# Loading an adjacency matrix transposed and checking it tile by tile in a four-layer graph kernel

## The chip, the core and the metric

The kernel runs on one core of a Trainium2 chip. The metric is the device time of one execution in microseconds (us), lower is better. The core has five engines, each with its own instruction stream: TensorE (PE; its weight loads are listed as PEld), VectorE (DVE), ScalarE (ACT), GpSimd (POOL) and SyncE (SP), which here issues all the DMAs. They meet only through semaphores. SBUF is the memory on the chip, with 128 partitions; PSUM is the memory that PE writes its products into, eight banks of 128x512 float32.

## What is computed

Four graph layers over `x` (8 graphs, 2048 nodes, 64 features) and one adjacency matrix `adj` (2048x2048), each with a residual and a layernorm. Cut to what matters:

```
# adj: 0/1 pattern with ones on the diagonal, each row divided by its sum
x = layernorm(x + L0(x, adj))   # x, A x and 2 A(A x) - x, mixed by weights made per node
x = layernorm(x + L1(x, adj))   # relu((A z) W), twice
x = layernorm(x + L2(x, adj))   # x Ws + (A x) Wn + bias
x = layernorm(x + L3(x, adj))   # [x, A x, 2A(Ax)-x, A x, 2A(Ax)-x] W + bias
```

All nonzero entries of row n are the same number r[n], the diagonal entry. So A is diag(r) times a 0/1 matrix, and the 0/1 matrix is exact in any format. Since this holds for the given matrix only, the kernel counts on the chip whether it does, and has a second, general body for any other matrix.

## The kernel before, in words

The eight graphs are four pairs j = 0..3 of 128 feature columns. A product of a pair with A is a pass p = 0..6 (0 and 1 for layer 0, 2 and 3 for layer 1, 4 for layer 2, 5 and 6 for layer 3). A pass has four chunks c of 512 nodes, a chunk is one PSUM bank: 16 blocks m of 128 nodes, for each a matmul of the high part and one of the low part of x (`xs`, split so that two fast fp32r matmuls give float32 accuracy) with the 0/1 matrix `B` (16 tiles of 128x2048). `mm` steps are quarters of a chunk, 8 matmuls. After a chunk DVE multiplies by `rrep`, which is r repeated over the partitions (step `scale`, L864); for p = 0 the result goes to memory (`y1d`) and, turned by four PE transposes (L571, step `after`) and copied by ACT (L727), back to the node-major form.

The **head** (L512 to L555 for PE and its counterparts `act_head`, `dve_head`, `pool_head`, `sp_head`) makes `B`. It loads `a` in 16 row tiles into four buffers, makes a 0/1 tile of each (`mb`: 768 columns on POOL, L983; 1280 on ACT, L674), turns it by 16 PE transposes (L530) and copies it from PSUM to `B` (ACT L693, DVE L813). DVE takes the diagonal (L798) and counts entries that differ from it (L803). `rrep` is made by matmuls with a matrix of ones (L545). Between the transposes PE makes pass 0 of pair 0 (128 matmuls, L559 and L560). At the end the counts are summed over the partitions by a matmul (L553), DVE writes `flag`, and every engine loads it and branches into `pe_main` and its counterparts.

Behind the branch every engine walks one list, `STEPS`, made by `order()` (L33) and written out by hand. It begins with the four `scale` and `after` steps of pass 0 of pair 0, which share one slot of `ring`, then `weights0` (the weights of layer 0, `Tw`), pass 1 of pair 0, and four quarters of pass 0 of pair 1. Then `opening(0)` prepares the operands of the per-node mixing of pair 0, and `weave` lays its 32 `T` steps (10 matmuls each, L653, and 8 DVE accumulations each, L965) among the quarters that pair 1 still has for layer 0: 28 of them, one between two `T` steps nearly everywhere. A `T` step takes one of two pairs of banks, so PE waits at a `T` until DVE has done the `T` before the last. Pairs 1, 2 and 3 follow in the same way, with the passes of the next pair among them, then the rest of the layers in two lanes.

Of the kernel before, what the change touches and what calls it, by code (L numbers as in the profile page):

```python
# [8 lines left out]
I32 = mybir.dt.int32  # L9
ALU = mybir.AluOpType  # L10
# [3 lines left out]
P = 128  # L14
# [7 lines left out]
NS = 768  # L22
# [10 lines left out]
def order():  # L33
# [5 lines left out]
    def one_pass(j, p):  # L39
# [12 lines left out]
        for c in range(NC):  # L52
            head = j == 0 and p == 0
            if not head:
                for m in range(4):
                    put("mm", j, p, c, m)
                    if c > 0 and p >= 2 and m == 0:
                        finish(c - 1)
                    if m < 3:
                        yield False  # L60
# [8 lines left out]
            if not head:  # L69
                yield True  # L70
# [72 lines left out]
    def layer0(j):  # L143
        yield from one_pass(j, 0)
        if j == 0:
            splits(j, 1)
            put("weights0")
        else:
            yield from split_ahead(j, 1)
        yield from one_pass(j, 1)  # L150

# [62 lines left out]
    for _ in layer0(0):  # L214
        pass
# [25 lines left out]


# [6 lines left out]
def gnn_stack(nc, xn, xt, a, at, emb, embt, b0, w01, w2, wbd, bias, eye, eps, out, zd, y1d, bd):  # L249
# [3 lines left out]
    with ctx:  # L253
# [5 lines left out]

        B = sb("B", [P, NT, N], F32R)  # L260
        with ExitStack() as scope:
            room = sb("room", [P, 2, N], F32, scope)
# [8 lines left out]
        r = sb("r", [P, NT], F32)  # L271
        cnt = sb("cnt", [P, NT], F32)
        neg = sb("neg", [P, NT], F32)
        sml = sb("sml", [P, 2, NC, 4, 8], F32)
        epst = sb("epst", [P, 1], F32)
        bad = sb("bad", [P, 1], F32)
        flag = sb("flag", [1, 1], I32)
        bias_t = sb("bias", [P, 2, C], F32)
        W1 = sb("W1", [P, 2, P], F32)
        with ExitStack() as scope:  # L280
            identb = sb("identb", [P, P], BF16, scope)
            onesf = sb("onesf", [P, P], F32, scope)
            mb0 = sb("mb0", [P, N], BF16, scope)
            astg = sb("astg", [P, N], F32, scope)
# [3 lines left out]
        with ExitStack() as scope:  # L288
            embn = sb("embn", [P, NT, DE], F32, scope)
            b0t = sb("b0t", [DE, C], F32, scope)  # L290
            with ExitStack() as inner:
                mb = [mb0, sb("mb1", [P, N], BF16, inner)]
            ring_x = sb("ring_x", [P, 2, 512], F32, scope)
# [4 lines left out]
        s_const, s_c2, s_w, s_x0, s_x1 = (sem(x) for x in ("const", "c2", "w", "x0", "x1"))  # L298
        s_a = [sem(f"a{i}") for i in range(4)]
        s_f = [sem(f"fetch{i}") for i in range(2)]  # L300
        s_p = sem("part")
        s_lx = [sem(f"loadx{i}") for i in range(2)]
        s_y1o = [sem(f"y1out{n}") for n in range(2)]
        s_z = [[sem(f"z{n}{c}") for c in range(NC)] for n in range(2)]
        s_re = [sem(f"reload{n}") for n in range(2)]
        s_out = [sem(f"out{n}") for n in range(2)]
        s_wl = sem("wload")
        s_e, s_bd = sem("embt"), sem("bd")
        s_g = [sem(f"g{i}") for i in range(2)]

        s_tr, s_rsum, s_sum, s_prod = sem("tr"), sem("rsum"), sem("sum"), sem("prod")
        s_turn, s_turny, s_four, s_b0, s_T = sem("turn"), sem("turny"), sem("four"), sem("b0"), sem("T")
        s_b0c = sem("b0copy")
        s_gmm = sem("gmm")

        s_signa, s_Ba, s_rrep, s_hi = sem("signa"), sem("Ba"), sem("rrep"), sem("hi")
        s_evict, s_sq, s_std, s_H, s_S, s_twh = (
            sem("evict"), sem("sq"), sem("std"), sem("H"), sem("S"), sem("twh"))
        s_gB = sem("gB")

        s_diag, s_cnt, s_Bd, s_lo, s_y, s_v = (
            sem("diag"), sem("cnt"), sem("Bd"), sem("lo"), sem("y"), sem("v"))
        s_flag, s_bad, s_chk = sem("flag"), sem("bad"), sem("chk")
        s_mean, s_var, s_norm, s_Lo, s_Sl = sem("mean"), sem("var"), sem("norm"), sem("Lo"), sem("Sl")
        s_acc, s_w0, s_twl, s_W = sem("acc"), sem("w0"), sem("twl"), sem("W")
        s_sum1, s_sum2, s_rec, s_Wc = sem("sum1"), sem("sum2"), sem("rec"), sem("Wc")
        s_ones_r, s_glo = sem("onesr"), sem("glo")

        s_ones, s_signp, s_join, s_pb = sem("ones"), sem("signp"), sem("join"), sem("pb")
# [3 lines left out]
        prod_at = {("prod", 0, 0, c): c + 1 for c in range(NC)}  # L333
        for s, v in numbered("mm", last=True).items():
            prod_at["prod", s.j, s.p, s.c] = v + 4
        split_at = {Step("split", j, 0, c): 4 * j + c + 1 for j in range(2) for c in range(NC)}
        split_at |= {s: v + 8 for s, v in numbered("split").items()}
        scale_at = numbered("scale")
        turn_at = numbered("ahead")
        turny_at = {s: i + 1 for i, s in enumerate(s for s in STEPS if s.kind == "after" and s.p in (0, 5))}  # L340
        four_at = {s: i + 1 for i, s in enumerate(s for s in STEPS if s.kind == "after" and s.p > 1)}
        evict_at = {s: i + 1 for i, s in enumerate(
            s for s in STEPS if s.kind == "ahead" or s.kind == "after" and s.p in (0, 2, 5))}
        v_at = {s: i + 1 for i, s in enumerate(s for s in STEPS if s.kind == "after" and s.p > 2)}
        pb_at = {s: i + 1 for i, s in enumerate(s for s in STEPS if s.kind == "after" and s.p in (4, 5))}
        T_at = numbered("T")
        join_at = numbered("join")
        prep_at = numbered("prep")
        prep2_at = {s: 2 * v for s, v in numbered("prep2").items()}
        mean_at, var_at, norm_at = numbered("centre"), numbered("deviate"), numbered("normed")  # L350
        n_T = len(T_at)

        def ahead(j, p, c):
            return Step("ahead", j, p, c)

        def after(j, p, c):
            return Step("after", j, p, c)


        load_at, load_after, slot_of = {}, {}, {}  # L360
        held, n_load = [None, None], [0, 0]
        for s in STEPS:
            if s.kind == "fetch" or s.kind == "part" and s.c % 2:
                i = s.p if s.kind == "fetch" else 1
                n_load[i] += 32 if s.kind == "fetch" else 16
                load_at[s], load_after[s], slot_of[s] = n_load[i], held[i], i
                held[i] = s


        bank_of, bank_after = {("prod", 0, 0, c): 4 + c for c in range(NC)}, {}  # L370
        turn, held = [0, 1], {}
        for i, s in enumerate(STEPS):
            if i == SECOND:
                turn = turn + [4, 5]
            if s.kind == "mm" and s.k == 0:
                b = turn.pop(0)
                turn.append(b)
                bank_of["prod", s.j, s.p, s.c], bank_after[s] = b, held.get(b)
                held[b] = Step("scale", s.j, s.p, s.c)
# [3 lines left out]
        nbank_of, nbank_after = {}, {}  # L383
        turn, held = [2, 3], {}

        def take(use, frees):
            b = turn.pop(0)
            turn.append(b)
            nbank_of[use], nbank_after[use] = b, held.get(b, (s_acc, 8 * n_T) if b > 3 else None)
            held[b] = frees  # L390

        for i, s in enumerate(STEPS):
            if i == SECOND:
                turn = turn + [6, 7]
            if s.kind == "ahead" or s.kind == "after" and s.p in (0, 5):
                take((s, "turn"), (s_evict, evict_at[s]))
            if s.kind == "after" and s.p == 2:
                take((s, "four"), (s_evict, evict_at[s]))
            if s.kind == "after" and s.p > 2:
                take((s, "four"), (s_v, v_at[s]))  # L400
# [3 lines left out]
        y_after, lx_at, lx_after, n_lx, n_y1o = {}, {}, {}, [0, 0], [0, 0]  # L404
        y1o_at = {}
        held = [[(s_rsum, 4)], [(s_rsum, 4)]]
        for s in STEPS:
# [9 lines left out]
            if s.kind == "loadx":  # L417
# [5 lines left out]
                elif s.j > 0:  # L423
                    lx_after[s] = (s_acc, 8 * T_at[Step("T", s.j - 1, 0, s.c + 2, 3)])
# [788 lines left out]
```

## Time and profile before

| | us |
|---|---|
| median of three runs | 1355.95 (1354.9 to 1357.07) |
| the profiled execution | 1359.67 |
| its span, first to last instruction | 1357.9 |
| PE busy | 1296.7 (95%) |
| DVE busy | 753.3 (55%) |
| ACT busy | 250.8 (18%) |
| POOL busy | 111.8 (8%) |

PE is busy 95% of the span, and 88% of the chain of work that ended last is PE's. The places where it isn't busy are read from stretches: a row of the table by stretches gives, for each engine, how long it was busy and with how many instructions, then the clock that TensorE was granted as a mean (1.00 is 2.4 GHz, 0.50 is 1.2 GHz), the share of the DMA engines and what they moved in GB/s. In the list in order of time a row is start, duration, engine, line, operation, output from inputs, shape, count, and in square brackets the idle time before it with what ended it.

### The profile page before, as it was taken

How to read it: one execution, taken by the hardware profiler on the slowest of the kernel's cores; microseconds unless marked ns; L12 is line 12 of the kernel's file. 1: busy time of each engine (PE TensorE's matmuls, PEld its weight loads, DVE VectorE, ACT ScalarE, POOL GpSimd, SP SyncE). 2: the span in 40 equal slices, each digit the busy share in tenths (PEclk: the TensorE clock that was granted, in tenths of full speed). 3: DMA queues.
4: the chain of work that ended last, by engine and by line, in shares of the span. 5: the costliest groups of instructions: out<-in, count | busy, mean ns of one | idle time of the engine just before them, and what ended most of it. 6: DMA issues, size and time to landing. Idle time of an engine off the chain costs nothing.

```text
span 1357.9 us, 16974 instructions
## 1 busy us (share of the span) xinstructions
PE 1296.7 (95%) x6314; PEld 1071.9 (79%) x6314; DVE 753.3 (55%) x1845; ACT 250.8 (18%) x433; POOL 111.8 (8%) x70
## 2 busy tenths in 40 slices
PE   6969999999999999799999999999999999999996
PEld 5758787778777888588888888888888888888885
DVE  6941677776777676866862453363135435334524
ACT  6730020111111120101111211121111211121211
POOL 5700000000000000000000101101000010010000
PEclk9979999999999999899999999999999999999998
DMA  8711111121112110100100000001001000000000
GB/s 303 290 58 39 27 56 36 47 73 36 47 35 74 36 59 24 47 28 20 39 14 1 1 1 0 1 8 55 1 9 55 0 1 1 1 1 0 32 1 34
DMA packets 25783, 54.06 MB, mean 40 GB/s; under 512 B 3024, under 2 KB 13776, under 8 KB 22992
## 3 DMA queue, kind: packets, MB, share of 16 engines
q1 hardware_dynamic: 25696, 52.90, 11.8%
q8 instruction: 54, 0.88, 0.3%
q14 instruction: 33, 0.27, 0.1%
HBM read 40.83 MB, written 12.06 MB: 39 GB/s over the span
## 4 chain that ended last, share of the span: by engine, by line
PE 88%; DVE 7%; DMA 2%; issue 1%; ACT 1%; POOL 1%; DVEq 0%; SPq 0%; ACTq 0%; POOLq 0%
PE ps L559 29%; PE ps L560 29%; PE ps L653 19%; PE ps L577 7%; PE ps L571 2%; DVE nat L965 1%; DVE ring L965 1%; DMA nat<-in_a 1%; DVE xs L875 1%; DVE xs L933 1%; DMA y1d<-ring 1%; PE ps L515 1%; POOL mb L983 1%; PE ps L530 0%; DVE nat L803 0%
## 5 line engine op out<-in xcount | busy, mean ns | idle before, releaser
L559 PE MATMUL ps<-B,xs 128*128 128x512 f32 x1792 | 712.3, 398 | 8.1 <-DVE xs L875 8.1
L560 PE MATMUL ps<-B,xs 128*128 128x512 f32 x1792 | 702.9, 392 | 0.0
L559 PEld LDWEIGHTS ps<-B,xs 128*128 128x128 f32 x1792 | 338.6, 189 | 78.4 <-issue 6.9
L560 PEld LDWEIGHTS ps<-B,xs 128*128 128x128 f32 x1792 | 338.7, 189 | 69.7
L653 PE MATMUL ps<-Tw,xs 128*128 128x512 f32 x1280 | 324.9, 402 | 15.3 <-DVE ring L965 7.8
L653 PEld LDWEIGHTS ps<-Tw,xs 128*128 128x128 f32 x1280 | 241.2, 191 | 77.7 <-DVE ring L965 9.7
L864 DVE TENSOR_TENSOR ring<-ps,rrep 128x512 f32<-128x512 f32 x96 | 66.3, 691 | 287.8 <-PE ps L560 275.6
L965 DVE SCALAR_TENSOR_TENSOR nat<-ps,embn,nat 128x128 f32<-128x128 f32 x448 | 154.1, 344 | 65.7 <-PE ps L653 65.7
L965 DVE SCALAR_TENSOR_TENSOR ring<-ps,embn,ring 128x128 f32<-128x128 f32 x512 | 175.5, 343 | 0.0
L577 PEld LDWEIGHTS ps<-W,ring 128*128 128x128 f32 x896 | 110.5, 191 | 7.0 <-DVE ring L864 2.6
L577 PE MATMUL ps<-W,ring 128*128 128x128 f32 x896 | 113.1, 275 | 1.7 <-DVE ring L864 1.7
L757 ACT ACTIVATE ring<-nat 128x512 f32<-128x512 f32 x60 | 37.9, 632 | 387.9 <-DVE nat L902 387.9
L1007 POOL TENSOR_TENSOR nat<-nat,bias 128x512 f32<-128x512 f32 x32 | 41.2, 1287 | 579.1 <-PE ps L571 579.1
L1000 POOL TENSOR_TENSOR nat<-nat,ring 128x512 f32<-128x512 f32 x16 | 23.6, 1476 | 596.9 <-DVE ring L965 596.9
L892 DVE TENSOR_TENSOR nat<-ps,nat 128x512 f32<-128x512 f32 x48 | 33.1, 690 | 66.6 <-PE ps L577 66.6
L965 DVE SCALAR_TENSOR_TENSOR nat<-ps,embn,ring 128x128 f32<-128x128 f32 x64 | 22.4, 350 | 79.5 <-PE ps L653 79.5
L762 ACT ACTIVATE sml<-sml,epst 128x8 f32<-128x8 f32 x64 | 19.3, 301 | 236.0 <-DVE sml L907 236.0
L752 ACT COPY ring<-ps 128x512 f32<-128x512 f32 x32 | 18.8, 587 | 177.4 <-PE ps L571 177.4
L875 DVE TENSOR_TENSOR xs<-nat,xs 128x512 fp32r<-128x512 f32 x64 | 40.2, 686 | 11.2 <-ACT xs L719 11.1
L902 DVE TENSOR_TENSOR nat<-nat,sml 128x512 f32<-128x512 f32 x64 | 44.4, 693 | 2.2
L912 DVE TENSOR_TENSOR nat<-nat,sml 128x512 f32<-128x512 f32 x64 | 44.3, 692 | 2.2
L907 DVE TENSOR_REDUCE sml<-ring 128x8 f32<-128x512 f32 x60 | 40.7, 678 | 8.4 <-ACT ring L757 8.4
(87 smaller groups left out, 601.3 us busy)
## 6 DMA issues: line engine op xcount, KB each, us to landing
room<-in_a SPq DMA_DIRECT2D x8, 1024.0 KB, 6.7
astg<-in_a SPq DMA_DIRECT2D x4, 1024.0 KB, 5.7
nat<-in_a SPq DMA_DIRECT2D x4, 1024.0 KB, 7.2
y1d<-ring SPq DMA_DIRECT2D x16, 256.0 KB, 2.4
ring<-in_xn SPq DMA_DIRECT2D x16, 256.0 KB, 2.9
ring_x<-in_xt SPq DMA_DIRECT2D x32, 128.0 KB, 3.2
ring_x<-y1d SPq DMA_DIRECT2D x32, 128.0 KB, 3.3
out<-nat SPq DMA_DIRECT2D x16, 256.0 KB, 2.4
```

The costliest lines, as they stand in the source:

```text
L559: pe.matmul(bank, x[:, 0, m, :], of, start=m == 0, stop=False)
L560: mm = pe.matmul(bank, x[:, 1, m, :], of, start=False, stop=ends and m == NT - 1)
L577: mm = pe.matmul(ps[:, bank, k * P:(k + 1) * P], src[:, k * P:(k + 1) * P], w, start=i == 0, stop=i == len(pairs) - 1)
L653: mm = pe.matmul(ps[:, 4 + 2 * p + q, :], src, Tw[:, wi, 512 * p:512 * p + 512], start=i == 0, stop=i == 4)
L757: ac.activation(square_slot(general, j, p, c), ch(nat[n], c), ACT.Square).then_inc(s_sq, 1)
L864: dv.tensor_tensor(to, ps[:, bank_of["prod", j, p, c], :], ch(rrep, 0 if general else c), ALU.mult).then_inc(s_y, 1)
L875: dv.tensor_tensor(lo, src, hi.bitcast(F32), ALU.subtract).then_inc(s_lo, 1)
L902: dv.tensor_tensor(g, g, sm[:, 1, :].unsqueeze(2).to_broadcast([P, 8, C]), ALU.subtract).then_inc(s_mean, 1)
L907: dv.tensor_reduce(sm[:, 2, :], q, axis=AX.X, op=ALU.add).then_inc(s_var, 1)
L912: dv.tensor_tensor(g, g, sm[:, 0, :].unsqueeze(2).to_broadcast([P, 8, C]), ALU.mult).then_inc(s_norm, 1)
L965: dv.scalar_tensor_tensor(sums[d % 2], ps[:, 4 + 2 * p:6 + 2 * p, i * C:(i + 1) * C], embn[:, t, d:d + 1], first[d] if d < 2 else sums[d % 2],
L1007: po.tensor_tensor(g, g, bias_t[:, p - 4, :].unsqueeze(1).to_broadcast([P, 8, C]), ALU.add).then_inc(s_pb, 1)
```

## The change

- **Loads.** The row tiles `a` are no longer an input. `adj.T` is loaded in 16 tiles `raw` into the place where `B` lies, without a wait between them. `rrep` and the diagonal come from the host as inputs of their own (`rb`, 1 MB, and `r16`). The pieces of x of pairs 0 and 1 are loaded ahead of every fourth tile.
- **Tile.** ACT counts the nonzero entries of a tile (Sign of its bits with `accum_out`); DVE compares the tile with `rrep`, writes the 0/1 result over it as `B` and counts the equal ones (`accum_out`). The transposes, the copies to `B`, POOL's part and the matmuls with ones are gone. The last tile is done in four pieces.
- **First products.** PE makes pass 0 of both pairs tile by tile in all eight banks: 16 matmuls for each tile. Chunks 2 and 3 of pair 1 are finished after tile 15, between the four `after` steps of pair 0. Each of the eight results has a slot of its own.
- **Outcome.** The difference of the two counts goes by DMA from a column to a row (`row<-bad`) while pass 1 of pair 0 runs; DVE writes `flag` after its eighth quarter, and all engines branch there.
- **Order.** `scale` and `after` of pair 1's pass 0 lie in pass 1 of pair 0, `weights0` behind the branch. Three quarters of pass 1 of pair 1 run ahead of the first `T`, and 13 are left to weave among the 32 `T` steps of pair 0.
- The general body starts from scratch and has semaphores of its own.

```diff
+    def head():
+        put("bias")
+        for m in range(NT):
+            if m % 4 == 0:
+                put("split", 0, 0, m // 4)
+                put("split", 1, 0, m // 4)
+            for c in range(NC if m == LAST else 1):
+                put("tile", 0, 0, c, m)
+            for j in range(2):
+                for c in range(NC if j == 0 else 2 if m >= 12 else NC):
+                    put("first", j, 0, c, m)
+            if m == LAST:
+                for c in range(NC):
+                    put("scale", 0, 0, c)
+        put("after", 0, 0, 0)
+        for m in range(12, NT):
+            put("first", 1, 0, 2, m)
...
+    def second_pass0():
+        products = one_pass(0, 1)
+        for i, _ in enumerate(products):
+            if i < 4:
+                put("scale", 1, 0, i)
+            if 2 <= i < 6:
+                put("after", 1, 0, i - 2)
+            if i == 7:
+                put("branch")
+                put("weights0")
+            if 8 <= i < 12:
+                put("split", 1, 1, i - 8)
...
-    products = layer0(1)
-    for _ in range(4):
-        next(products)
     put("loadx", 0, 0, 0)
     put("fetch", 0, 0, 0)
+    products = one_pass(1, 1)
+    for _ in range(3):
+        next(products)
     opening(0)
-    weave(0, products, 30, 2, 3)
+    weave(0, products, 13, 2, 3)
...
+                    if s.kind == "first" and not general:
+                        bank, of = ps[:, bank_of["prod", j, 0, c], :], B[:, k, c * 512:(c + 1) * 512]
+                        pe.wait_ge(s_B, tile_at[Step("tile", 0, 0, c if k == LAST else 0, k)])
...
+                        pe.matmul(bank, xs[n][:, 0, k, :], of, start=k == 0, stop=False)
+                        mm = pe.matmul(bank, xs[n][:, 1, k, :], of, start=False, stop=k == LAST)
...
+                        ac.activation(junk[:, tile_at[s] % 2, cols], raw[:, k, cols].bitcast(U32), ACT.Sign,
+                                      accum_out=cnt[:, 1, k + c:k + c + 1]).then_inc(s_nz, 1)
...
+                        dv.wait_ge(s_nz, tile_at[s])
+                        dv.scalar_tensor_tensor(B[:, k, cols], raw[:, k, cols], 1.0, rrep[:, cols], ALU.mult, ALU.is_equal,
+                                                accum_out=cnt[:, 0, k + c:k + c + 1]).then_inc(s_B, 1)
...
+                    if s.kind == "branch" and not general:
+                        dv.wait_ge(s_row, 16)
+                        dv.tensor_reduce(worst[:], row[:], axis=AX.X, op=ALU.max).then_inc(s_chk, 1)
+                        dv.wait_ge(s_chk, 3)
+                        dv.tensor_copy(flag[:], worst[:]).then_inc(s_flag, 1)
...
+                    if s.kind == "weights0":
+                        sp.wait_ge(s_y1o[0], 64)
+                        sp.wait_ge(s_turny, turny_at[after(0, 0, 3)])
+                        sp.dma_start(w01s, w01).then_inc(s_w, 16)
+                        sp.dma_start(w2s, w2).then_inc(s_w, 16)
```

What stands in a row at three places, first before and then with the change. **DVE at the end of the head**; `astg`, `nat` and `room` hold row tiles before, `raw` is a transposed tile, L803 and L816 are the counts:

```order
L798 SCALAR_TENSOR_TENSOR ring,r<-room,identf 128x128
L803 SCALAR_TENSOR_TENSOR room,cnt<-room,r,mb 128x2048
L813 CAST B<-ps 128x8x128
L818 TENSOR_TENSOR xs<-nat,xs 128x512 x4
L820 TENSOR_SCALAR neg<-r 128x16
L822 TENSOR_TENSOR cnt<-cnt,neg 128x16
L824 TENSOR_REDUCE bad<-cnt 128x1
```

```order
L854 TENSOR_TENSOR xs<-nat,xs 128x512 x2
L816 SCALAR_TENSOR_TENSOR B,cnt<-raw,rrep 128x2048 x3
L816 SCALAR_TENSOR_TENSOR B,cnt<-raw,rrep 128x512 x4
L842 TENSOR_TENSOR ring<-ps,rrep 128x512 x4
L854 TENSOR_TENSOR xs<-nat,xs 128x512 x4
L821 TENSOR_TENSOR odd<-cnt 128x19
```

Each tile now has one DVE instruction where it had two and, for every second tile, a copy (L813). The last tile has four short ones, and the scalings of pair 0 (L842) follow on them ahead of the sums for `flag`.

**DVE around the branch**, from the end of the head to the weights of layer 0 (`Tw`):

```order
L826 TENSOR_SCALAR bad<-ps 1x1
L828 CAST flag<-bad 1x1
L1145 TENSOR_LOAD flag
L1145 ISA x2
L1146 COMPARE_AND_BRANCH
L864 TENSOR_TENSOR ring<-ps,rrep 128x512 x4
L875 TENSOR_TENSOR xs<-nat,xs 128x512 x4
L916 TENSOR_TENSOR ring<-ring 64x1024
```

```order
L842 TENSOR_TENSOR ring_x<-ps,rrep 128x512
L842 TENSOR_TENSOR nat<-ps,rrep 128x512
L827 TENSOR_REDUCE worst<-row 1x1
L829 CAST flag<-worst 1x1
L1139 TENSOR_LOAD flag
L1139 ISA x2
L1140 COMPARE_AND_BRANCH
L895 TENSOR_TENSOR ring<-ring 64x1024
L897 TENSOR_SCALAR ring<-ring 128x1024
```

The scaling and splitting that stood behind the branch stand ahead of it, and the reduction for `flag` follows directly on the scaling of chunk 1 of pass 1 of pair 0 (`nat<-ps,rrep`).

**DVE at the opening**, from the last scalings of pass 1 of pair 0 to the first `T` (L965 before, L944 now):

```order
L864 TENSOR_TENSOR nat<-ps,rrep 128x512 x4
L864 TENSOR_TENSOR ring<-ps,rrep 128x512
L933 TENSOR_TENSOR xs<-nat,xs 64x512 x2
L943 TENSOR_TENSOR xs<-ring_x,xs 128x512
L965 SCALAR_TENSOR_TENSOR nat<-ps,embn,ring 128x128
```

```order
L854 TENSOR_TENSOR xs<-nat,xs 128x512
L842 TENSOR_TENSOR nat<-ps,rrep 128x512
L912 TENSOR_TENSOR xs<-nat,xs 64x512 x2
L922 TENSOR_TENSOR xs<-ring_x,xs 128x512
L944 SCALAR_TENSOR_TENSOR nat<-ps,embn,ring 128x128
```

The scaling into `ring`, that of pair 1's chunk 0 in pass 0, which stood between the last scaling of pair 0 and the preparation, is no longer there.

## Rows read from the trace of the kernel before

**Rows 1.** By stretches: us, busy PE, PEld, DVE, ACT, POOL, clock, DMA share, GB/s.

```profile
0.00:82.90 82.90, 65.62 (x426) 52.28 (x426) 61.69 (x85) 50.69 (x54) 47.03 (x22) 0.94 0.69 254
82.90:96.70 13.80, 4.43 (x16) 2.88 (x17) 3.60 (x6) 3.82 (x8) 0.00 (x0) 0.52 0.20 76
96.70:134.90 38.20, 38.19 (x160) 31.27 (x160) 8.62 (x11) 4.98 (x8) 0.00 (x0) 0.95 0.11 35
134.90:138.00 3.10, 0.15 (x1) 0.00 (x0) 2.75 (x4) 0.00 (x0) 0.00 (x0) 1.00 0.00 0
138.00:271.20 133.20, 130.32 (x560) 104.48 (x560) 93.69 (x296) 18.20 (x32) 3.88 (x3) 0.99 0.15 41
271.20:1357.90 1086.70, 1057.97 (x5152) 881.01 (x5152) 582.97 (x1445) 173.11 (x333) 60.92 (x45) 0.99 0.07 23
```

**Rows 2.** In order of time, the first 12 us.

```profile
3.77 7.08 PE L515 MATMUL ps<-b0t,ring 16*128 16x64 f32 x32 [3.77 <-DMA b0t<-in_b]
...
7.78 2.79 POOL L983 TENSOR_SCALAR mb<-astg 128x768 bf16<-128x768 f32 x1 [3.19 <-DMA astg<-in_a]
...
10.89 1.01 ACT L678 COPY rrep<-ps 128x1024 f32<-128x1024 f32 x1 [8.89 <-PE ps L515]
```

**Rows 3.** Busy time by stretches, ten microseconds in the head.

```profile
10.00:20.00 10.00, 5.68 (x45) 4.68 (x46) 6.75 (x8) 8.48 (x8) 7.15 (x4) 1.00 1.01 389
```

**Rows 4.** Single lines: ns least/median/most, first and last start in us.

```profile
L803 DVE SCALAR_TENSOR_TENSOR room<-room,r,mb x8: 2352/2352/2904, 20.1 to 70.1; 128x2048 f32<-128x2048 f32 x8
L798 DVE SCALAR_TENSOR_TENSOR ring<-room,identf x8: 274/284/289, 19.8 to 69.8; 128x128 f32<-128x128 f32 x8
L873 DVE SCALAR_TENSOR_TENSOR xs<-stg,xs x12: 683/687/693, 765.2 to 1119.1; 128x512 fp32r<-128x512 f32 x12
L674 ACT ACTIVATE mb<-room x8: 1270/1274/1292, 16.1 to 66.2; 128x1280 bf16<-128x1280 f32 x8
```

**Rows 5.** In order of time, PE at the start of pass 1 of pair 0.

```profile
96.71 0.76 PE L559 MATMUL ps<-B,xs 128*128 128x512 f32 x1 [2.11 <-DVE xs L875]
...
100.86 0.39 PE L559 MATMUL ps<-B,xs 128*128 128x512 f32 x1
```

**Rows 6.** In order of time, PE's transposes of one chunk.

```profile
158.85 0.60 PE L571 MATMUL ps<-identf,ring 128*128 128x128 f32 x4
159.20 1.18 PE L653 MATMUL ps<-Tw,xs 128*128 128x512 f32 x4
```

**Rows 7.** In order of time, DVE at the branch.

```profile
83.10 0.69 DVE L864 TENSOR_TENSOR ring<-ps,rrep 128x512 f32<-128x512 f32 x1 [1.13 <-issue]
```

**Rows 8.** In order of time, DVE on the weights of layer 0.

```profile
98.28 1.21 DVE L916 TENSOR_TENSOR ring<-ring 64x1024 f32<-64x1024 f32 x1
...
103.50 1.22 DVE L922 TENSOR_TENSOR Tw<-ring,Tw 128x1024 fp32r<-128x1024 f32 x1
```

**Rows 9.** In order of time, PE before the first `T`.

```profile
134.43 0.39 PE L559 MATMUL ps<-B,xs 128*128 128x512 f32 x1
134.66 0.39 PE L560 MATMUL ps<-B,xs 128*128 128x512 f32 x1
138.03 8.96 PE L653 MATMUL ps<-Tw,xs 128*128 128x512 f32 x30 [2.99 <-DVE xs L943]
```

**Rows 10.** In order of time, `T` steps on DVE and PE.

```profile
142.18 0.35 DVE L965 SCALAR_TENSOR_TENSOR nat<-ps,embn,ring 128x128 f32<-128x128 f32 x1 [4.25 <-PE ps L653]
142.45 0.34 DVE L965 SCALAR_TENSOR_TENSOR ring<-ps,embn,ring 128x128 f32<-128x128 f32 x1
...
240.81 2.50 PE L653 MATMUL ps<-Tw,xs 128*128 128x512 f32 x10
244.98 2.50 PE L653 MATMUL ps<-Tw,xs 128*128 128x512 f32 x10
```

**Rows 11.** In order of time, PE's last `T` steps of pair 0.

```profile
267.92 2.59 PE L653 MATMUL ps<-Tw,xs 128*128 128x512 f32 x10 [1.41 <-DVE ring L965]
271.28 4.90 PE L653 MATMUL ps<-Tw,xs 128*128 128x512 f32 x20 [0.78 <-DVE ring L965]
```

More of the change, by code:

```diff
@@ L52, in one_pass @@
         for c in range(NC):
[L53 to L60, printed above, removed]
+            for m in range(4):
+                put("mm", j, p, c, m)
+                if c > 0 and p >= 2 and m == 0:
+                    finish(c - 1)
+                if m < 3:
+                    yield False
             if c > 0 and p < 2:
@@ L68, in one_pass @@
                 put("normed", j, p, 2)
[L69 to L70 removed]
+            yield True
         put("after", j, p, 3)
@@ L144, in layer0 @@
         yield from one_pass(j, 0)
[L145 to L149, printed above, removed]
-        yield from one_pass(j, 1)
+        yield from split_ahead(j, 1)
+        yield from one_pass(j, 1)
+    def head():
[15 more added lines that the diff above has]
+            put("first", 1, 0, 2, m)
+        put("after", 0, 0, 1)
+        put("split", 0, 1, 0)
+        put("after", 0, 0, 2)
+        put("split", 0, 1, 1)
+        for m in range(12, NT):
+            put("first", 1, 0, 3, m)
+        put("after", 0, 0, 3)
+        put("split", 0, 1, 2)
+        put("split", 0, 1, 3)
+        put("flag")
+    def second_pass0():
[10 more added lines that the diff above has]
+                put("split", 1, 1, i - 8)
     def layer1(j):
@@ L337, in gnn_stack @@
[L337 to L370, printed above, removed]
@@ L376, in gnn_stack @@
                 b = turn.pop(0)
                 turn.append(b)
[L378 to L400, printed above, removed]
@@ L703, in act_main @@
-        def act_main(ac, general):
-            if general:
-                ac.wait_ge(s_prod, 4)
+                nbank_of[use], nbank_after[use] = b, held.get(b, (s_acc, 8 * n_T))
+                held[b] = frees
+            for i, s in enumerate(STEPS):
+                if i == SECOND:
+                    turn = turn + [6, 7]
+                if s.kind == "after" and s.p == 0 and s.j < 2:
+                    nbank_of[s, "turn"] = bank_of["prod", s.j, 0, s.c]
+                    nbank_after[s, "turn"] = None
+                elif s.kind == "ahead" or s.kind == "after" and s.p in (0, 5):
+                    take((s, "turn"), (s_evict, evict_at[s]))
+                if s.kind == "after" and s.p == 2:
+                    take((s, "four"), (s_evict, evict_at[s]))
+                if s.kind == "after" and s.p > 2:
+                    take((s, "four"), (s_v, v_at[s]))
@@ new lines, in pe_quarter, with pe_rest @@
+            def pe_quarter(pe, x, bank, c, k, ends):
+                for m in range(4 * k, 4 * k + 4):
+                    of = B[:, m, c * 512:(c + 1) * 512]
+                    pe.matmul(bank, x[:, 0, m, :], of, start=m == 0, stop=False)
+                    mm = pe.matmul(bank, x[:, 1, m, :], of, start=False, stop=ends and m == NT - 1)
+                return mm
+            def pe_rest(pe, x, bank, v):
+                for m in range(NT):
+                    pe.wait_ge(s_glo, 16 * (v - 1) + m + 1)
+                    pe.matmul(bank, x[:, 0, m, :], glo[:], start=False, stop=m == NT - 1).then_inc(s_gmm, 1)
@@ new lines, in pe_turned, with pe_weighed @@
+            def pe_turned(pe, bank, src):
+                for k in range(4):
+                    mm = pe.transpose(ps[:, bank, k * P:(k + 1) * P], src[:, k * P:(k + 1) * P], identf[:])
+                return mm
+            def pe_weighed(pe, bank, *pairs):
+                for k in range(4):
+                    for i, (src, w) in enumerate(pairs):
+                        mm = pe.matmul(ps[:, bank, k * P:(k + 1) * P], src[:, k * P:(k + 1) * P], w,
+                                       start=i == 0, stop=i == len(pairs) - 1)
+                return mm
@@ new lines, in pool_steps @@
+            def pool_steps(po, steps):
+                for s in steps:
+                    j, p, c, k, n = s.j, s.p, s.c, s.k, s.j % 2
+                    g = groups(nat[n], c)
+                    if s.kind == "join":
+                        po.wait_ge(s_acc, 8 * T_at[Step("T", j, 1, c, 3)])
+                        po.tensor_tensor(ch(nat[n], c), ch(nat[n], c), ring[:, c % 2, :], ALU.add).then_inc(s_join, 1)
+                    if s.kind == "after" and p in (4, 5):
+                        po.wait_ge(s_turn, turn_at[ahead(j, p, c)])
+                        po.wait_ge(s_norm, norm_at[Step("normed", j, p - 1, c)])
+                        po.wait_ge(s_hi, split_at[Step("split", j, p, c)])
+                        po.wait_ge(s_lo, split_at[Step("split", j, p, c)])
+                        po.wait_ge(s_c2, 48)
+                        po.tensor_tensor(g, g, bias_t[:, p - 4, :].unsqueeze(1).to_broadcast([P, 8, C]),
+                                         ALU.add).then_inc(s_pb, 1)
```

1382 lines of the change are left out of this document (658 added, 724 removed).

## The prediction

> **What bounds the kernel now.** I read the stretches first [rows 1]. PE is the bound wherever it has work: from 96.7 to 134.9 us it is busy 38.19 of 38.20, from 138.0 to 271.2 it is busy 130.3 of 133.2, and behind 271.2, where the change touches nothing, 1058 of 1087. What is left to gain lies ahead of 138 us. In the first 82.9 us PE shows 65.6 us busy, but with the transposes and with matmuls at the lower clock; the useful part of that is pass 0 of pair 0, 128 matmuls. From 82.9 to 96.7 PE is busy 4.4 of 13.8 us, because four chunks go one after the other through one slot. From 134.9 to 138.0 it stands still for 3 us.
>
> So the reader is to see two prices. A product matmul starts every 0.227 us at 2.4 GHz (134.43, 134.66) [rows 9], so 128 of them are 29.1 us. And everything up to 96.7 us yields only those 29.1 us of products.
>
> **Method.** I build the new course of PE up to the first `T` of pair 1, which begins at 271.3 us now [rows 11]. The order behind it is the same, so what is gained there is the gain.
>
> **Start of the products.** Three chains meet.
> - Load. The first row tile landed at 7.78 us [rows 2]. In front of the first transposed tile stand in addition four times 128x512 and once 128x2048 in float32 less two, that is 0.5 MB of x and 1 MB of `rb`. At 389 GB/s [rows 3] 1.57 MB take 4.0 us: tile 0 is there at 11.8.
> - ACT. The bias product began at 3.77, took 7.1, and the copy followed at 10.89 for 1.01 [rows 2]. Its operands now come behind two loads of x; I put 1.7 us on it, so ACT is free at 13.6. Two casts of x over 512 columns, at L674's rate 0.5 each and a little more, bring it to 14.7. Then Sign over 2048 columns: L674 takes 1.27 for 1280 [rows 4], at the same rate 2.0. It ends at 16.7.
> - DVE. Compare and count over 2048 columns: L803 has 2.35 [rows 4]. It ends at 19.1.
>
> PE starts at 19.2 us, and ACT, not the load, sets it.
>
> **Pace of the head.** Per tile: load 1.05 MB at 389 GB/s, 2.7 us; ACT 2.0; DVE 2.35, with the splits of x (0.69 each, as L873 [rows 4], two for every four tiles) 2.7; PE 16 matmuls, 3.6 us. PE is the slowest, so load, count and compare are hidden behind it, by 0.9 us a tile. At 0.43 us each (the lower level, below) PE takes 6.8 and is hidden even less. POOL does nothing. If DVE's instruction took over 3.3 us this cover would be gone; that is the first rival.
>
> **Sum for PE.**
> 1. Start 19.2.
> 2. 256 first matmuls at 0.227: 58.2, so 77.4.
> 3. At the start PE comes from a pause, on its lower level of 1.2 GHz. After the pause of 2.1 us ahead of 96.71 the first matmuls were so, and at 100.86 they were at full rate [rows 5]; nine matmuls by 0.2 more are 1.8. I add 1.8: 79.2. Twice as much is possible.
> 4. Four `after` steps of pair 0: the transposes at 158.85 delayed the next work to 159.20 [rows 6], 0.4 each, 1.6: 80.8. Between them lie 16 matmuls (3.6 us), against 0.69 of scaling, so no wait.
> 5. Pass 1 of pair 0, 128 matmuls, 29.1, and pair 1's four `after` steps, 1.6: 111.5. The stall of 82.9 to 96.7 is gone, since each result has a slot and a bank of its own.
> 6. Branch. PE has to wait until DVE has scaled chunk 1, which it completed itself: 0.69 for the scaling, 0.4 for the reduction and the cast (two small instructions, an estimate), then from the end of the cast to the next instruction 1.13 [rows 7], and about 0.2 because the last matmul runs on 0.16 us past the next one's place: 2.4. Whether the clock falls after such a pause, the rows leave open: a pause of 2.99 at 138.03 was followed by 30 matmuls in 8.96 us instead of 7.0 [rows 9], one of 1.41 was not (10 in 2.59) [rows 11]. I take half of 1.7, 0.8: 114.7. Before, the branch lay in time in which PE had nothing to do anyway; its price is new.
> 7. Three quarters of pass 1 of pair 1, 5.5: 120.2. First `T`, against 138.0. They cover the 2.8 us of preparation on DVE that stalled PE at 134.9 [rows 1, 9], since the scaling of pair 1 that stood ahead of it is gone.
> 8. A `T` and a quarter take 4.17 (240.81 to 244.98) [rows 10], less 1.82 for the quarter: 2.35. 32 `T` are 75.2, 13 quarters 23.7: 219.1.
> 9. Waits among the `T`, 5.0, and 1.4 that my prices leave unexplained in the same stretch before: 225.5.
>
> The same prices applied to the old stretch give 28 quarters, 51.0, 32 `T`, 75.2, four `after`, 1.6, clock 1.7 and waits 2.4, together 131.9 against 133.3; that is the 1.4.
>
> The 5.0: at the end of pair 0 five `T` stand without a quarter. With the end of the last quarter at 0, PE would reach the next pair's first `T` at 11.7. DVE does a `T` in 2.07 (8 by 0.26 [rows 10]) and has besides the scaling, the deviation, a norming, the two preparations and two splits, about 6.4, ahead of the `T` before last: it is done with that at 16.8. PE waits 5.1, against 1.4 and 0.8 now [rows 11]. Elsewhere a quarter stands after every second `T`: PE has 2 x 2.35 + 1.82 = 6.5, DVE 2 x 2.07 and on average 1.5 of other work, 5.6, and I find no wait there.
>
> 225.5 against 271.3 is a gain of 45.8. The profiled execution had 1359.67 us, its span 1357.9, and the median 1355.95; the execution would come to 1313.9 and the median to **1310**.
>
> **Weights.** Moved behind the branch, their loads are issued there by SP. They need about 5 us to land (an estimate: 1 MB at 389 GB/s and some 2 us), their work on DVE and ACT 6.4 (98.28 to 104.7 [rows 8]), then the splits 2.8: 14.2 us after the branch. PE has eight quarters, 14.6, ahead of the first matmul that needs a split of pair 1, and three more ahead of `T`. The first `fetch` is queued behind that on SP and lands at about 17, against 20. Cost nothing, with about 2 us of cover; beyond that each us costs one.
>
> **Rivals.**
> - **DVE sets the pace of the head.** L816 reads two float32 tiles from SBUF and accumulates. The rows speak against a lower rate: L873 reads two such tiles, 512 columns in 0.687, L798 reads two and accumulates, 128 in 0.284, and L803, where the second is bf16, does 2048 in 2.352 [rows 4]; all three are columns by 1.04 ns and 0.15 to 0.2. But none has all at 2048 columns. At half the rate a tile would take 2.35 + 2.1 = 4.5, fifteen of them with splits and the last in pieces would end at 93 instead of 57, PE's head at 100 instead of 81: gain 27, time 1329. The Trainium skill says in "Vector Engine (DVE) Microarchitecture Reference", section 7, Points that are easy to get wrong, that this form with two non-bf16 SBUF sources halves throughput, since both read ports are used and none is left for the accumulator. By that rule, the trace disagrees as far as L798 shows. Chance 8%.
> - **The thinner weave doesn't cover DVE.** The product quarters among the `T` steps fall from 28 to 13. DVE has 93.7 us busy in that stretch [rows 1], less some 4.7 for three scalings and four splits that now come earlier: 89 of PE's 99. If its bunches (centring 1.6, preparing 1.4) met the gaps, each of the six half chunks in which they stand would give a wait like the 1.41 [rows 11], 8.4 in all, or the weights would land late by some us: 1318 to 1320. Chance 17%.
> - **The general body runs.** If one of the 19 pairs of counts differed, all would be redone with 16 more matmuls in each of 112 chunks, 112 x 16 x 0.227 = 407 us, on top of the 97 us spent: above 1800, slower than before. It decides from a single count that differs. The same matrix passes a count now, since no row of the general body is in the trace; against it stands that Sign is taken of the bits. Chance 2%.
>
> **Numbers.** Forecast 71%, from 1303 (start at 17, no fall of the clock, few waits) to 1317 (start at 21, lower clock twice as long, a longer branch); rivals 8, 17 and 2%; 2% for a head of another kind, such as slow loads, that ends within 0.2%. The range of 80% is 1302 to 1326; it takes in the thin weave and stops short of the half rate. 0.2% (2.7 us) is about what a measurement can tell from no change. Faster 0.96, same 0.02, slower 0.02.
>
> **What would show it.** Right: the first product matmul near 19 us and no waits of PE on DVE or loads until about 80; L816 at 2.3 to 2.4 us; a pause of 2.4 us after the eighth quarter of pass 1; first `T` near 120, first `T` of pair 1 near 225, and the same 1087 us behind it. Wrong: L816 above 3.3 us, a pause at the first split or `T` of pair 1 (late weights), or waits of PE on L944 above 8 us within pair 0.

## The result, and the profile after

The kernel with the change takes 1313.74 us (median of four runs, 1312.39 to 1315.02) against 1356.51 for the kernel before: ratio 0.968, 95% interval 0.966 to 0.970. Measured again beside the experiments it was 1313.09 against 1357.04, ratio 0.967 (0.966 to 0.969). The profiled execution took 1312.39 us, its span 1310.5. The forecast was 1310, 43 to 44 us of gain against the 45.8 forecast.

By stretches, with the columns of [rows 1] (duration, busy time of PE, PEld, DVE, ACT, POOL, clock, DMA share, GB/s); the cuts are the start of the products, the end of the four transposes of pair 0, the pause at the branch, the first `T`, and the first `T` of pair 1:

```profile
core 0: us, PE busy (x) PEld busy (x) DVE busy (x) ACT busy (x) POOL busy (x), PEclk, DMA share, GB/s
0.00:20.10 20.10, 7.10 (x33) 6.91 (x33) 3.66 (x5) 7.71 (x9) 0.20 (x4) 1.00 0.87 319
20.10:82.60 62.50, 62.50 (x272) 51.58 (x273) 40.95 (x48) 33.42 (x45) 0.00 (x0) 1.00 0.63 251
82.60:99.40 16.80, 16.74 (x83) 13.51 (x81) 5.28 (x12) 3.97 (x7) 0.00 (x0) 1.00 0.19 63
99.40:101.60 2.20, 0.00 (x0) 0.02 (x1) 0.99 (x3) 0.00 (x0) 0.00 (x0) 1.00 0.00 0
101.60:121.60 20.00, 19.99 (x88) 16.58 (x89) 10.04 (x13) 7.70 (x12) 0.00 (x0) 1.00 0.42 126
121.60:226.10 104.50, 101.86 (x425) 79.25 (x424) 88.50 (x288) 12.52 (x22) 3.89 (x3) 0.99 0.14 42
226.10:1310.50 1084.40, 1057.12 (x5154) 880.34 (x5152) 581.87 (x1445) 172.99 (x333) 61.89 (x45) 0.99 0.07 23
```

From 20.1 us on PE is busy without a gap to the branch, where the kernel before had its two stretches of 82.9 and 13.8 us. The clock column reads 1.00 for 20.1 to 82.6 us, but the first 13 product matmuls follow each other at 0.43 us and not at 0.227, the lower level, until 25.8:

```profile
24.95 0.63 PE L620 MATMUL ps<-B,xs 128*128 128x512 f32 x1
25.37 0.57 PE L619 MATMUL ps<-B,xs 128*128 128x512 f32 x1
25.78 0.40 PE L620 MATMUL ps<-B,xs 128*128 128x512 f32 x1
```

Behind the first `T` of pair 1 (226.1 is worked out from the rows around it, a matmul or two either way) stand 1084 us where 1087 stood. So the gain was made ahead of that place: 271.3 less 226.1 is 45.2 us. The 2.2 behind it are no effect of the change (see the account of the prediction).

How the products start, in order of time:

```profile
6.55 7.08 PE L609 MATMUL ps<-b0t,ring 16*128 16x64 f32 x32 [6.55 <-DMA b0t<-in_b]
...
13.67 1.01 ACT L706 COPY bcopy<-ps 128x1024 f32<-128x1024 f32 x1 [11.66 <-PE ps L609]
...
15.62 1.91 ACT L712 ACTIVATE junk<-raw 128x2048 bf16<-128x2048 uint32 x1
...
17.73 2.29 DVE L816 SCALAR_TENSOR_TENSOR B<-raw,rrep 128x2048 fp32r<-128x2048 f32 x1 [1.13 <-ACT junk L712]
...
20.09 0.79 PE L619 MATMUL ps<-B,xs 128*128 128x512 f32 x1 [6.45 <-DVE B L816]
```

PE waits for DVE, DVE for ACT, ACT for PE's bias product, and that for its operands: the forecast's chain, 0.9 us later. The counts of one line tell what a compare costs:

```profile
L816 DVE SCALAR_TENSOR_TENSOR B<-raw,rrep x19: 689/2289/2294, 17.7 to 58.3; 128x2048 fp32r<-128x2048 f32 x15, 128x512 fp32r<-128x512 f32 x4
```

The last compare starts at 58.3, and PE has first products until 82. In all of 24 to 226 us PE has two kinds of pause, at the branch and at the last `T` steps of pair 0:

```profile
101.61 0.47 PE L580 MATMUL ps<-B,xs 128*128 128x512 f32 x1 [2.27 <-issue]
```

```profile
222.79 8.81 PE L689 MATMUL ps<-Tw,xs 128*128 128x512 f32 x30 [2.46 <-DVE ring L944]
232.20 2.59 PE L689 MATMUL ps<-Tw,xs 128*128 128x512 f32 x10 [0.60 <-DVE ring L944]
```

These answer to [rows 11]: the wait ahead of the last `T` of pair 0 is 2.46 where it was 1.41. The first row also shows the lower clock, 30 matmuls in 8.81 us where 7 would do.

### The profile page after: what moved, and what is told of

Its sections match the earlier page's. It is cut to its first block, busy times and chain, and to the rows that moved or that the text cites. A ratio compares the mean times of both kernels' runs of the same rounds, so it can differ in the third digit from the quotient of the medians.

```text
span 1310.5 us, 16451 instructions
## 1 busy us (share of the span) xinstructions
PE 1265.3 (97%) x6048; PEld 1048.2 (80%) x6048; DVE 731.3 (56%) x1811; ACT 238.3 (18%) x427; POOL 66.0 (5%) x52
## 3 DMA queue, kind: packets, MB, share of 16 engines
q1 hardware_dynamic: 27424, 53.96, 11.9%
## 4 chain that ended last, share of the span: by engine, by line
PE 92%; DVE 6%; issue 1%; ACT 1%; DMA 1%; SPq 0%; DVEq 0%; ACTq 0%
PE ps L580 28%; PE ps L581 28%; PE ps L689 20%; PE ps L598 7%; PE ps L619 2%; PE ps L620 2%; PE ps L592 2%; DVE nat L944 1%; DVE ring L944 1%; PE ps L609 1%; DVE xs L912 0%; DMA b0t<-in_b 0%; DVE xs L854 0%; DVE xs L922 0%; DMA W<-in_wbd 0%
## 5 line engine op out<-in xcount | busy, mean ns | idle before, releaser
L580 PEld LDWEIGHTS ps<-B,xs 128*128 128x128 f32 x1664 | 313.2, 188 | 72.7 <-issue 9.2
L581 PEld LDWEIGHTS ps<-B,xs 128*128 128x128 f32 x1664 | 313.2, 188 | 64.1
L842 DVE TENSOR_TENSOR ring<-ps,rrep 128x512 f32<-128x512 f32 x94 | 64.5, 690 | 287.5 <-PE ps L581 269.7
L944 DVE SCALAR_TENSOR_TENSOR nat<-ps,embn,nat 128x128 f32<-128x128 f32 x448 | 154.2, 344 | 57.9 <-PE ps L689 57.5
L944 DVE SCALAR_TENSOR_TENSOR ring<-ps,embn,ring 128x128 f32<-128x128 f32 x512 | 175.7, 343 | 0.0
L854 DVE TENSOR_TENSOR xs<-nat,xs 128x512 fp32r<-128x512 f32 x72 | 45.5, 686 | 28.7 <-ACT xs L722 28.3
L765 ACT ACTIVATE sml<-sml,epst 128x8 f32<-128x8 f32 x64 | 19.2, 301 | 231.5 <-DVE sml L886 231.5
L944 DVE SCALAR_TENSOR_TENSOR nat<-ps,embn,ring 128x128 f32<-128x128 f32 x64 | 22.4, 350 | 67.7 <-PE ps L689 67.6
L881 DVE TENSOR_TENSOR nat<-nat,sml 128x512 f32<-128x512 f32 x64 | 44.4, 693 | 2.2
```

Of the source, the lines that this page charges most:

```text
L580: pe.matmul(bank, x[:, 0, m, :], of, start=m == 0, stop=False)
L581: mm = pe.matmul(bank, x[:, 1, m, :], of, start=False, stop=ends and m == NT - 1)
L842: dv.tensor_tensor(to, ps[:, bank_of["prod", j, p, c], :], ch(rrep, 0 if general else c), ALU.mult).then_inc(s_y, 1)
L854: dv.tensor_tensor(lo, src, hi.bitcast(F32), ALU.subtract).then_inc(s_lo, 1)
L881: dv.tensor_tensor(g, g, sm[:, 1, :].unsqueeze(2).to_broadcast([P, 8, C]), ALU.subtract).then_inc(s_mean, 1)
L944: dv.scalar_tensor_tensor(sums[d % 2], ps[:, 4 + 2 * p:6 + 2 * p, i * C:(i + 1) * C], embn[:, t, d:d + 1], first[d] if d < 2 else sums[d % 2],
```

## The experiments

### Which part sets the head: every compare twice

The theory is that PE paces the head and hides DVE's 2.3 us a tile behind its own 3.6. The test makes DVE the slower one and changes nothing else.

```diff
+                        dv.scalar_tensor_tensor(extra[:, cols], raw[:, k, cols], 1.0, rrep[:, cols], ALU.mult,
+                                                ALU.is_equal).then_inc(s_extra, 1)
                         dv.scalar_tensor_tensor(B[:, k, cols], raw[:, k, cols], 1.0, rrep[:, cols], ALU.mult, ALU.is_equal,
```

> The change, with every compare of a tile on DVE done twice (the first result goes to an unused place). Theory: PE paces the head with 3.6 us a tile and DVE hides behind it with 2.3; at 4.6 DVE is the pace, 15 tiles and the splits end at 90 and the last tile at 95, so the four transposes of pair 0 end at about 101 instead of 83 and the kernel takes 18 us more than the change (16 to 20). Rival: another thing, the loads or the count on ACT, sets the head, or the head's end is not on the path; then it takes 0 to 3 us more.

1331.59 us against 1313.09, 18.5 more. PE's waits from the start to 300 us, what for, total, times, longest:

```profile
PE ps L621 <- DVE B L824: 20.1, 14, 8.6
PE ps L611 <- DMA b0t<-in_b: 6.3, 1, 6.3
PE ps L691 <- DVE ring L954: 3.1, 2, 2.5
PE ps L582 <- issue: 2.3, 1, 2.3
```

and the last transposes of pair 0's pass 0, which began at 82.26 in the change:

```profile
98.79 0.60 PE L594 MATMUL ps<-identf,ring 128*128 128x128 f32 x4
```

14 waits for the compare where there was one. The head ends 16.5 us later, less than the 18 expected: DVE took 4.41 us for a tile and not 4.6, since its instructions overlap by 0.08. In this execution 1.7 more come from the branch, where the clock fell to 1.2 GHz for 3.4 us behind the pause, which it did not in the profiled executions of the change (below); whether it did in the other executions behind the medians is not known. The loads and the count stayed as they were, so they don't set the head; PE does, up to somewhere between 2.3 and 4.4 us of DVE per tile.

### One part alone: four slots in the kernel before

```diff
+        def y_slot(j, p, c):
+            if j == 0 and p == 0:
+                return [ring[:, 4, :], ring[:, 5, :], ring_x[:, 0, :], ring_x[:, 1, :]][c]
+            return ring[:, 4 + j % 2, :]
...
-                        to = ring[:, 4 + n, :]
+                        to = y_slot(j, p, c)
```

> The kernel before, with four slots instead of one for the scaled chunks of pass 0 of pair 0. Theory: the pause from 82.9 to 96.7 us is the wait of each scaling for the DMA that empties the slot; with four slots pass 1 begins at about 88.5 and the kernel takes 8 us less than before (ratio 0.994). Rival: the weights of layer 0 and the first fetch come too late for the earlier T, and the 8 us turn up as a wait at the first T of pair 0: ratio 1.000.

1348.83 us, 8.2 less than before, ratio 0.994 (0.992 to 0.996). The four scalings now follow each other, the four transposes too, and pass 1 begins at 89.4 instead of 96.7:

```profile
82.98 1.29 DVE L876 TENSOR_TENSOR ring<-ps,rrep 128x512 f32<-128x512 f32 x2 [1.13 <-issue]
...
84.18 1.28 DVE L876 TENSOR_TENSOR ring_x<-ps,rrep 128x512 f32<-128x512 f32 x2
...
89.40 0.47 PE L569 MATMUL ps<-B,xs 128*128 128x512 f32 x1 [2.11 <-DVE xs L887]
```

So of the 44 us a fifth is this alone, and could have been had with fewer than twenty lines. The first matmul behind the shorter pause takes 0.47, not 0.76 as in [rows 5]: the granted clock was at half from 84.2 us for 3.4 us and had risen again by then, where in the kernel before it was low from 83.5 for 17.1 us, the first 3.9 us of pass 1 among them. So the first `T` comes 9.1 us earlier (128.9 against 138.0), 7.3 by the shorter pause and 1.9 by the clock. It still waits 2.99 us, as before.

### What the second pair in the head is worth

```diff
-            for j in range(2):
-                for c in range(NC if j == 0 else 2 if m >= 12 else NC):
-                    put("first", j, 0, c, m)
+            for c in range(NC):
+                put("first", 0, 0, c, m)
...
-    products = one_pass(1, 1)
+    products = layer0(1)
...
-    weave(0, products, 13, 2, 3)
+    weave(0, products, 31, 2, 3)
```

The rest of that edit gives pair 1's chunks their old banks and slot.

> The change, but only pair 0's first products in the head; those of pair 1 are made as before, in 13 + 16 quarters among the T steps after three ahead of them. Theory: the head is then paced by loads and DVE (2.7 us a tile) and ends near 60 us instead of 83, PE idles in it, and the 16 quarters (29 us) come back in the weave: first T of pair 0 near 100 instead of 122, first T of pair 1 near 233 instead of 226, 6 to 8 us slower than the change. Rival A: the second pair in the head is worth its full 29 us. Rival B: it is worth nothing, since the thin weave makes PE wait for DVE; then this version is within 2 us of the change or faster.

1319.40 us, 6.3 more than the change. By stretches, cut at the start of the products, of pass 1, near the first `T` (102.6) and the first `T` of pair 1 (234.9):

```profile
20.10:63.80 43.70, 35.92 (x144) 25.94 (x145) 40.75 (x47) 33.32 (x46) 0.00 (x0) 1.00 0.90 358
63.80:102.00 38.20, 35.85 (x150) 29.26 (x151) 11.69 (x19) 7.10 (x12) 0.00 (x0) 0.96 0.20 65
102.00:234.90 132.90, 130.73 (x572) 105.18 (x571) 94.26 (x297) 17.07 (x30) 3.88 (x3) 1.00 0.14 42
```

With one pair the head is short, because DVE (40.75 of 43.70) and the loads (0.90) fill it, and PE waits. The head and pass 1 are done 19 us earlier than in the change (102.6 against 121.7 at the first `T`), and 28 come back in the weave (132.3 against 104.5), which leaves 8.8 at the first `T` of pair 1 (6.3 by the medians). Of the 8.8, 1.7 are a fall of the clock behind the pause at the branch, which the change's profiled execution was spared. The second pair fills PE's idle time, 7.8 us of the 43.7 here, and that, not its 29 us of matmuls, is its worth. Both halves of the sum were forecast, and the rival of the thin weave falls: with 13 quarters PE is busy 101.9 of 104.5 us there.

This run also tells what became of the pause of 82.9 to 96.7 us. Here nothing of pair 1 lies between the four `after` steps, and yet pass 1 begins only 3.4 us after the last product of the head, which starts at 60.39:

```profile
60.63 2.03 PE L581 MATMUL ps<-identf,ring 128*128 128x128 f32 x16
...
63.82 0.47 PE L569 MATMUL ps<-B,xs 128*128 128x512 f32 x1 [1.16 <-DVE xs L843]
```

In the kernel before it is 15.6 us (81.10 to 96.71, with the branch between them), with four slots alone 8.4 (80.98 to 89.40). So the slots took away 7.2 us, and 5.0 went with the rest of the new order: the branch no longer stands ahead of the scaling, and the clock stays up. No run takes these two apart, and 2.3 us come back at the branch's new place. Only the last 1.16 of waiting was left for the products of pair 1 to cover.

### The branch

```diff
-            if i == 7:
+            if i == 6:
                 put("branch")
```

> The change, with the branch one quarter earlier, so that DVE's two small instructions for the flag stand ahead of the scaling of chunk 1 and need nothing that PE has just made. Theory: of the pause of 2.27 us at the branch 1.3 is the chain of scaling, reduction and cast on DVE, and it goes; what is left is the load of the flag and the branch, which PE's matmuls in flight may hide: 0 to 1.0 us. Time 1.3 to 2.3 us less than the change. Rival: the pause is the refill of instructions at a branch and stays at 2.3 us wherever the flag is made.

1311.00 us, ratio 0.966 (0.964 to 0.967), 2 us less than the change by the medians, which the intervals don't separate; the trace does. (This run and the three below were measured in a second group, beside the kernel before at 1357.13 us but not beside the change, which they are compared with over the groups.) PE's waits as they are listed for 21 to 240 us; the first is the wait for the first compare, ahead of the products' start at 20.2 us, which the list still counts:

```profile
PE ps L619 <- DVE B L816: 6.4, 1, 6.4
PE ps L689 <- DVE ring L944: 3.1, 2, 2.5
```

Two waits at the `T` steps, 3.1 us together, are all that is left beside the start; around the branch PE is busy throughout:

```profile
96.00:101.00 5.00, 5.00 (x23) 4.13 (x22) 1.91 (x2) 0.82 (x2) 0.00 (x0) 1.00 0.41 166
```

Loading the flag and branching cost PE nothing when the flag is there. PE's instruction stream runs ahead of its matmuls and loads the flag at 94.0 us, while the last matmul ahead of the branch starts at 97.4:

```profile
L1115 PEldq TENSOR_LOAD <-flag x1: 484/484/484, 94.0 to 94.0; - x1
```

In the change the same load starts at 100.5, since the flag is there only at 100.42, behind the scaling of what PE had just made. Of its 2.27 us of pause 1.1 are that wait for the flag and 1.2 the load and the branch behind it. The forecast had the size right and both parts, 1.13 for the second; moving the flag removes both, where the expectation above left the second open.

### The quarters one step later

```diff
-    weave(0, products, 13, 2, 3)
+    weave(0, products, 13, 2, 2)
```

> The change, with the 13 quarters spread to one T step later and the preparation of pair 1 behind that. Theory: the wait of 2.46 us at the last T of pair 0 comes from five T without a quarter and DVE's other work among them, and it brings the fall of the clock at 223.9 us; with one quarter between them the wait goes below 1 us, the clock stays at 2.4 GHz and the time is 2 to 4 us less than that of the change. Rival: the wait moves to the first T of pair 1, whose operands are prepared later, and nothing is gained.

1312.24 us, ratio 0.967 (0.965 to 0.968): no gain that can be told. The wait moved to the first `T` of pair 1, as the rival said:

```profile
219.93 2.60 PE L689 MATMUL ps<-Tw,xs 128*128 128x512 f32 x10 [0.31 <-DVE ring L944]
225.45 10.04 PE L689 MATMUL ps<-Tw,xs 128*128 128x512 f32 x30 [2.92 <-DVE ring L944]
```

DVE has the same accumulations, preparation and splits to do ahead of it. The run doesn't tell quite the whole, since in its profiled execution the clock fell behind the pause at the branch:

```profile
100.40:106.00 5.60, 5.55 (x17) 4.45 (x18) 0.87 (x1) 0.00 (x0) 0.00 (x0) 0.70 0.56 187
```

where the change, after as long a pause at as good as the same place, shows

```profile
101.60:107.00 5.40, 5.39 (x24) 4.47 (x25) 0.67 (x1) 0.00 (x0) 0.00 (x0) 1.00 0.58 194
```

24 matmuls against 17 in about the same time; 3.4 us at half the clock cost 1.7 us. Such a fall came in three of the profiled executions with this pause (also with every compare twice and with one pair in the head) and stayed away in three (the change twice, and the next experiment).

### The start

```diff
+        put("tile", 0, 0, 0, 0)
         put("bias")
         for m in range(NT):
...
-            for c in range(NC if m == LAST else 1):
+            for c in range(NC if m == LAST else 1 if m else 0):
...
+                sp.dma_start(embt_s, embt).then_inc(s_e, 16)
+                sp.dma_start(b0t[:], b0).then_inc(s_e, 16)
                 for c in range(NC):
```

> The change, with the loads of the bias product first, and on ACT and DVE the count and compare of tile 0 ahead of the copy of the bias product and of the splits of x. Theory: ACT's chain of bias copy, two casts and count sets PE's start at 20.1 us; with the count first the start is 15.6 to 17 us and the whole kernel 3 to 4.5 us faster than the change. Rival: tile 0 lands only shortly before 15.6 us, when its count began in the change, so the load sets the start and it stays within 1 us of 20.1.

1308.88 us, ratio 0.965 (0.963 to 0.966), 4.2 us less than the change by the medians.

```profile
11.93 1.91 ACT L713 ACTIVATE junk<-raw 128x2048 bf16<-128x2048 uint32 x1 [9.91 <-DMA raw<-in_at]
...
14.04 2.29 DVE L817 SCALAR_TENSOR_TENSOR B<-raw,rrep 128x2048 fp32r<-128x2048 f32 x1 [14.04 <-ACT junk L713]
...
16.26 1.29 DVE L855 TENSOR_TENSOR xs<-nat,xs 128x512 fp32r<-128x512 f32 x2
...
17.09 0.76 PE L620 MATMUL ps<-B,xs 128*128 128x512 f32 x1 [5.82 <-DVE xs L855]
```

Tile 0 was there at 11.9 us (11.8 forecast), so ACT had been the chain. PE starts 3.0 us earlier, just outside the 15.6 to 17 expected: the splits on DVE now stand behind the compare and end last. The pause at the branch ends 2.5 and 3.4 us earlier than in the two profiled executions of the change; what the medians have beyond that is not resolved.

### All three

```diff
+        put("tile", 0, 0, 0, 0)
         put("bias")
...
-            for c in range(NC if m == LAST else 1):
+            for c in range(NC if m == LAST else 1 if m else 0):
...
-            if i == 7:
+            if i == 6:
                 put("branch")
...
-    weave(0, products, 13, 2, 3)
+    weave(0, products, 13, 2, 2)
...
+                sp.dma_start(embt_s, embt).then_inc(s_e, 16)
+                sp.dma_start(b0t[:], b0).then_inc(s_e, 16)
                 for c in range(NC):
```

> The change with all three edits: branch earlier, quarters one T later, tile 0 first. Theory: the gains lie at different places of PE's course and add up: 6 to 10 us less than the change, ratio to the kernel before 0.960 to 0.963. Rival: the earlier PE arrives at the first T of pair 0 or at the splits of pair 1, the more it waits there for the weights of layer 0, and less than 4 us remain.

1305.88 us, ratio 0.962 (0.961 to 0.963), 7.2 to 7.9 us below the change and faster than both kernels. The three taken alone gave 2.1, 4.2 and 0.9 by the medians, together 7.2. That this meets 7.2 so closely is in part luck, since the first and the last of them lie within the noise; but nothing says that they take from each other, and no wait for the weights appeared. PE's last wait is the one that only moved:

```profile
218.37 8.96 PE L690 MATMUL ps<-Tw,xs 128*128 128x512 f32 x30 [2.92 <-DVE ring L945]
```

The change once more, as the control of the first group:

> The changed kernel once more, beside the other kernels of this group. Both theories: the first T of pair 1 at 226 us, ratio to the kernel before 0.968, within 0.003.

1313.09 us, ratio 0.967 (0.966 to 0.969). The last `T` of pair 0 starts at 221.96 us behind a wait of 2.47, so the first of pair 1 follows near 225.9. At the start only 9 matmuls ran at the lower clock, and the branch came 0.85 us earlier than in the first profiled execution.

## Why the prediction was right, step by step

| step | forecast | measured |
|---|---|---|
| start of the products | 19.2 | 20.1 |
| end of pair 0's transposes | 80.8 | 82.6 |
| pause at the branch | 2.4, and 0.8 for the clock | 2.27, no fall of the clock |
| first `T` of pair 0 | 120.2 | 121.7 |
| first `T` of pair 1 | 225.5 | 226.1 |
| behind it | 1086.6 | 1084.4 |

The places agree within 2 us, but in part because errors cancel: the head ended 1.8 late, the clock that did not fall at the branch gave back 0.8, and the weave was 0.8 shorter.

- **What bounds it** held. The head was PE's, and doubling DVE's part moved its end by 16.5 us, where the sum of the instructions said 18.
- **Start.** The chain was right and 0.9 late: the bias product's operands landed at 6.55, not 5.5, a 4 KB load behind half a megabyte of x. The price of its place in the queue was the mis-sized term, 2.8 us instead of 1.7.
- **Lower clock at the start.** 13 matmuls at 0.43 cost 2.7 us more than at the full rate, not 1.8. With the start this is the whole 1.8 by which the head ended late. The number varies by the execution: 9 in the second one of the change, 7 to 13 over all eight with the new head. The forecast's nine lay within that.
- **Removed pause.** Taken as gone with its 13.8 us, and it was. The forecast gave a slot and a bank for each result as the reason; that is half of it. Four slots alone gave 7.3 us at the start of pass 1 and 8.2 in time, the scaling ahead of the branch and the full clock most of the rest (the run with one pair in the head), and the products of pair 1 covered the last 1.2.
- **Branch.** Right in size, with the parts shown above. The open half, whether the clock falls, stays open run by run; that it did not fall here is luck.
- **Weights.** Forecast: done 14.2 us behind the branch, with about 2 us of cover. Measured: DVE started on them at 106.3, was through at 112.7, and the fourth split of pair 1 was done at 115.8, 14.2 us behind the 101.6 at which PE went on. The first split, the one that PE asked for at 116.2, was done at 113.4. The cover was 2.8.
- **Weave.** 104.5 us against the forecast 105.3. Only the 5.0 of waits at its end was a little high: 2.46, and 1.2 for the lower clock behind it, which lasted from 223.7 to 227.1 us and so cost 0.5 more behind 226.1.
- **The rival of the half rate** fell in the first trace: a compare of 2048 columns took 2.289 us, less than L803's 2.352 [rows 4], so two float32 sources and the accumulator cost nothing here. The Trainium skill's sentence on it (Vector Engine (DVE) Microarchitecture Reference, section 7, Points that are easy to get wrong) is not borne out by this form.
- **The profiled executions** make the gain 47.3 us, the medians 43 to 44. The profiled one of before, 1359.67, was slower than all other executions of that kernel, and the first one of the change the fastest of its four. The 2.2 us behind 226.1 come of this. In the kernel before one instruction of DVE took 1.71 us and its three equals 0.68, and PE's next wait was 1.67 us:

```profile
273.41 1.71 DVE L875 TENSOR_TENSOR xs<-ring_g,xs 128x512 fp32r<-128x512 f32 x1 [0.21 <-ACT xs L719]
277.84 2.60 PE L653 MATMUL ps<-Tw,xs 128*128 128x512 f32 x10 [1.67 <-DVE ring L965]
```

  With four slots, in the same order of steps, that wait is 0.35 us, and in the change 0.60. And behind the two long waits near 562 and 574 us the clock stayed low for 6.8 and 3.4 us, in the change's profile behind the same two (517 and 528) for 3.4 and 3.4; its second profile has 3.4 and 6.8. That is 1.1 and 1.7 us, less the 0.5 named under the weave: 2.3. None of this is in the forecast's 45.8, which lies ahead of the place. Of the 2 to 3 us by which the medians stay below 45.8, 0.6 stand in the table (226.1 against 225.5) and 0.5 are that fall of the clock; the rest has no place yet.

## What to carry to other kernels

Price a kernel's opening by the work of the bounding engine that it yields per microsecond, not by that engine's busy time: the head here showed PE busy and produced 29 us of products in 97. To fill such a stretch, bring in work that needs nothing but what is being loaded, and count what it leaves uncovered later; 29 us moved forward were worth 6. A flag that all engines branch on should be made from things that were finished long ago: then the branch cost PE nothing here. And compare one profiled execution with another only with care: one long instruction and one longer fall of the clock made nearly 3 of the 47.3 us between these two.

## What was not expected of the hardware

- After pauses of PE of 2.2 to 2.3 us the granted clock fell to 1.2 GHz for 3.4 us in three profiled executions and not in three others, at the same place of nearly the same program. After the 21 pauses of 2.46 to 3.22 us in the ten traces it fell every time, at the latest 1.3 us behind the pause; after the waits of 1.41 to 1.47 us at the `T` steps and the late splits it did not.
- The load of a register from SBUF and the branch took 1.0 us on SP and 1.2 on PE from the end of the cast to their next work, and left no gap on PE when the flag was set ahead of time.
- With about ten loads outstanding SP needed up to 4.1 us to issue one (a 64 KB load at 9.37 us), yet the loads kept moving, at 416 GB/s in these 4.1 us and at 414 to 421 between 20 and 50 us.
